# A recurrent block behind a cross-attention layer: another loop order, another end, and the last channel mixing on ScalarE and GpSimd

## The reference

```python
xa = ln(x, ln1);  sx = previous(xa) - xa
xxx = tanh((xa + sx * maa_x) @ maa_w1)             # the mixer
xk, xw, xv, xr, xg = xa + sx * (maa_stack + xxx @ maa_w2)
w = exp(-exp(time_decay + tanh(xw @ td_w1) @ td_w2));  r, k, v = ...
scan over t:  out = r . (u*k*v + s);  s = k*v + w*s  # 32 heads of 8
x1 = x + (group_norm(out) * silu(xg @ Wg.T)) @ Wo.T
xc = ln(x1, ln2);  sx2 = previous(xc) - xc           # the channel mixing
xk2 = xc + sx2 * ffn_maa_k;  xr2 = xc + sx2 * ffn_maa_r
return x1 + sigmoid(xr2 @ Wfr.T) * (square(relu(xk2 @ Wfk.T)) @ Wfv.T)
```

## Time and profile before

| | us |
|---|---|
| median of 3 runs (1112.25 to 1114.79) | 1112.68 |
| the profiled execution, its whole time | 1108.56 |
| its span | 1106.8 |
| busy: PE / DVE / ACT / POOL | 1051.5 / 888.8 / 768.4 / 607.8 |

### The profile page before, as it was taken

How to read it: one execution, slowest core, us unless ns; L and a number is a source line. 1 busy time by engine, 2 the same in 40 slices (tenths; PEclk the granted TensorE clock), 3 DMA queues, 4 the chain that set the end, 5 groups by cost and what they waited for, 6 DMA issues and landing times.

```text
span 1106.8 us, 34650 instructions
## 1 busy us (share of the span) xinstructions
PE 1051.5 (95%) x12992; PEld 878.5 (79%) x12992; DVE 888.8 (80%) x1532; ACT 768.4 (69%) x1910; POOL 607.8 (55%) x535
## 2 busy tenths in 40 slices
PE   5899999999999998999999999999999999887888
PEld 4888989888988987877788887777887777665677
DVE  5997777978777777128999999999999999999543
ACT  5677877777777776566666676666677667744774
POOL 4787888777887786024443454443454443453322
PEclk9999999999999999999999999999999999999999
DMA  9500000011111110012333331233331233303011
GB/s 331 177 4 2 0 0 2 4 41 41 41 41 46 38 38 12 1 38 70 72 81 86 86 73 45 59 81 85 85 78 38 57 83 86 86 25 99 21 38 57
DMA packets 39868, 65.01 MB, mean 59 GB/s; under 512 B 4384, under 2 KB 26208, under 8 KB 39392
## 3 DMA queue, kind: packets, MB, share of 16 engines
q1 hardware_dynamic: 39776, 63.75, 21.7%
HBM read 55.35 MB, written 8.39 MB: 58 GB/s over the span
## 4 chain that ended last, share of the span: by engine, by line
PE 84%; DVE 8%; issue 3%; ACT 3%; POOL 1%; DMA 0%; DVEq 0%; ACTq 0%; POOLq 0%
PE psum L1016 10%; PE psum L1005 10%; PE psum L353 10%; PE psum L1097 9%; PE psum L267 6%; PE psum L336 5%; PE psum L368 5%; PE psum L297 4%; PE psum L280 3%; PE psum L1056 3%; PE psum L1136 2%; PE psum L310 2%; PE psum L1169 2%; PE psum L1278 2%; DVE shared L1839 2%
## 5 line engine op out<-in xcount | busy, mean ns | idle before, releaser
L1839 DVE TENSOR_TENSOR_SCAN shared<-late_wT,shared 128x512 f32<-128x512 f32 x128 | 193.8, 1514 | 0.0
L232 POOL TENSOR_TENSOR shared<-shared,att_row_max 128x512 f32<-128x512 f32 x128 | 132.6, 1055 | 16.8 <-DVE att_row_max L564 16.8
L453 ACT ACTIVATE shared<-shared 128x512 f32<-128x512 f32 x128 | 80.5, 631 | 68.3 <-POOL shared L232 68.2
L353 PE MATMUL psum<-shared 128*128 128x128 f32 x1024 | 126.1, 277 | 0.1
L353 PEld LDWEIGHTS psum<-shared 128*128 128x128 f32 x1024 | 120.4, 193 | 0.5 <-ACT shared L462 0.5
L1016 PE MATMUL psum<-w,late_hT 128*128 128x256 f32 x512 | 120.0, 382 | 0.5 <-ACT late_hT L1396 0.5
L564 DVE TENSOR_REDUCE att_row_max<-shared 128x8 f32<-128x512 f32 x128 | 86.8, 680 | 40.9 <-POOL shared L225 40.9
L1005 PE MATMUL psum<-late_glnT,w 128*128 128x256 f32 x512 | 118.0, 383 | 1.1 <-ACT late_glnT L1387 1.0
L896 POOL TENSOR_TENSOR late_xm<-late_mixed,late_xa 128x512 f32<-128x512 f32 x64 | 78.1, 1229 | 72.6 <-DVE late_mixed L1805 72.6
L905 POOL TENSOR_TENSOR shared<-shared,late_rT 128x512 f32<-128x512 f32 x32 | 40.7, 1273 | 122.8 <-DVE shared L1839 122.8
L1005 PEld LDWEIGHTS psum<-late_glnT,w 128*128 128x128 f32 x512 | 94.7, 190 | 16.8 <-issue 3.2
(11 more groups left out here) (169 smaller groups left out, 2470.8 us busy)
## 6 DMA issues: line engine op xcount, KB each, us to landing
shared<-v_rows SPq DMA_DIRECT2D x64, 512.0 KB, 7.7
shared<-in_enc SPq DMA_DIRECT2D x64, 128.0 KB, 2.6
v_rows<-shared SPq DMA_DIRECT2D x64, 64.0 KB, 1.8
out<-x SPq DMA_DIRECT2D x16, 256.0 KB, 2.0
x<-in_x SPq DMA_DIRECT2D x7, 512.0 KB, 9.8
w<-in_w SPq DMA_DIRECT2D x2, 1024.0 KB, 17.2
shared<-in_cross_mask SPq DMA_DIRECT2D x1, 1024.0 KB, 12.3
shared<-in_w_qkv SPq DMA_DIRECT2D x1, 768.0 KB, 4.6
```

The source lines that it names most:

```text
L232: nc.gpsimd.tensor_tensor(zs, zs, peak.unsqueeze(2).to_broadcast([P, PAIRS, S]), ALU.subtract).then_inc(shifted, 1)
L353: last = nc.tensor.matmul(dst[:, half * P:(half + 1) * P], w[:, kb, c0 + half * P:c0 + (half + 1) * P], src[:, u % 2, kb, 0:P], start=(kb ...
L453: nc.scalar.activation(probs[:, u % 2, half * 4:(half + 1) * 4, :].rearrange("p r k -> p (r k)"), z[:, u % 2, half, :], ACT.Exp).then_inc( ...
L1839: nc.vector.tensor_tensor_scan(states, wT[:, u, half, :, :, :].rearrange("p j b t -> p (j b t)"), states, 0.0, ALU.mult, ALU.add).then_inc ...
```

## The change

1. **Loop order** (bodies 0 to 12). TensorE does `mixer(s+1)` right behind the gate's projection and no longer behind the head sums, the bonus sums and the output projection. VectorE does `mixer_input(s+1)` ahead of the first scan. ScalarE takes the mixer's tanh ahead of setting two groups of first states.
2. **Channel mixing in bodies 13 to 15.** For runs 0 to 5 `ch_mix` on VectorE is gone. ScalarE makes the four products (`ch_scale`), GpSimd the two additions (a `ch_mix` of its own). From run 6 on VectorE does it as before.
3. **The end.** `centre(14)`, `sum_squares(14)`, `square(14)`, the moments of run 13 and `scale(14)` move from behind the bodies into body 15. Behind the bodies the recurrence's last pieces come earlier. ScalarE makes the group norm's roots for runs 14 and 15 apart, each with two table loads, and the second `NORMS` group now takes runs 10 to 13, the last one only 14 and 15.

```diff
-        NORMS = ((0, (RUNS - 6) * CH), ((RUNS - 6) * CH, (RUNS - 3) * CH), ((RUNS - 3) * CH, RUNS * CH))
+        NORMS = ((0, (RUNS - 6) * CH), ((RUNS - 6) * CH, (RUNS - 2) * CH), ((RUNS - 2) * CH, RUNS * CH))
...
+                ch_mix(early_run(s, 0), 0)
...
+            if n == 4 and early(s):
+                ch_mix(early_run(s, 1), 1)
...
-        if there(s - 1) and not s_is(s, RUNS - 1):
-            scale(s - 1)
...
+        if there(s - 1):
+            scale(s - 1)
...
+    def ch_mix(r, u):
+        pool.wait_ge(ch_scaled, r + 1)
+        for dst in (ch_xk, ch_xr):
+            xs = dst[:, u, :, :].rearrange("p h (b t) -> p (h b) t", t=S)
+            last = nc.gpsimd.tensor_tensor(xs, xs, ch_xc[:, u, :, :, 1:S + 1].rearrange("p h b t -> p (h b) t"),
+                                           ALU.add)
+        last.then_inc(ch_mixed_ready, 1)
+
...
     ch_add(EARLY - 1, 1)
+    scale(RUNS - 1)
...
-    scale(RUNS - 2)
-    scale(RUNS - 1)
     ch_add(EARLY, 0)
...
     ch_add(EARLY + 1, 1)
-    ch_shift(EARLY + 4, 0)
-    ch_add(EARLY + 2, 0)
-    channel(EARLY + 3, 1)
-    channel_runs(pool, channel)
+    channel_runs(pool, channel, EARLY + 2)
...
+        if mixing and not early(s):
+            mixer(s + 1)
...
-        if mixing:
+        if mixing and early(s):
             mixer(s + 1)
...
-    ch_keys(EARLY, 0)
...
+    ch_keys(EARLY, 0)
+    transpose_on(RUNS - 2)
+    transpose_o(RUNS - 1)
...
-    transpose_o(RUNS - 1)
+    project_out(RUNS - 2)
...
-    ch_transpose(EARLY + 3, 1)
-    ch_keys(EARLY + 2, 0)
-    transpose_on(RUNS - 2)
-    ch_values(EARLY + 1, 1)
-    ch_receptances(EARLY + 2, 0)
-    project_out(RUNS - 2)
-    ch_transpose(EARLY + 4, 0)
-    ch_keys(EARLY + 3, 1)
...
-    ch_values(EARLY + 2, 0)
-    ch_receptances(EARLY + 3, 1)
+    channel(EARLY + 1, 1)
...
-    channel(EARLY + 3, 1)
-    channel_runs(pe, channel)
+    channel_runs(pe, channel, EARLY + 2)
...
+    def ch_scale(r, u):
+        act.wait_ge(ch_sx_ready, r + 1)
+        if r == 0:
+            act.wait_ge(down_ready, RUNS)
+        if later(r - 1):
+            act.wait_ge(ch_key_ready, r - 1)
+            act.wait_ge(ch_recept_ready, r - 1)
+        for half in range(HALVES):
+            for dst, name in ((ch_xk, "ffn_maa_k"), (ch_xr, "ffn_maa_r")):
+                last = nc.scalar.activation(dst[:, u, half, :].rearrange("p (b t) -> p b t", t=S),
+                                            ch_sx[:, u, half, :, :], ACT.Copy, scale=col(core, name, half))
+        last.then_inc(ch_scaled, 1)
+
...
-        if there(s - 1) and there(s):
+        if early(s):
             set_states(s, 2)
             set_states(s, 3)
+        if early(s):
+            ch_scale(early_run(s, 0), 0)
...
             mixer(s + 1)
+        if there(s - 1) and there(s) and not early(s):
+            set_states(s, 2)
+            set_states(s, 3)
...
+            ch_scale(early_run(s, 1), 1)
             ch_tanh(early_run(s, 0), 0)
-        if there(s - 2) and not s_is(s, RUNS - 1):
+        if there(s - 2):
             out_means(s - 2)
-        if there(s - 1) and not s_is(s, RUNS - 1):
+        if there(s - 1):
             square(s - 1)
...
-    square(RUNS - 2)
+    nc.scalar.preload_act_table_set("natural_log_exp_and_others")
+    invert_heads(RUNS - 2)
+    ch_invert(1)
+    nc.scalar.preload_act_table_set("gelu_apprx_tanh_and_others")
...
+    copy_on(RUNS - 2)
...
+    square(RUNS - 1)
+    nc.scalar.preload_act_table_set("natural_log_exp_and_others")
+    invert_heads(RUNS - 1)
+    nc.scalar.preload_act_table_set("gelu_apprx_tanh_and_others")
...
-    ch_square(EARLY + 1, 1)
-    make_stats(RUNS - 3)
-    square(RUNS - 1)
-    nc.scalar.preload_act_table_set("natural_log_exp_and_others")
-    invert_heads(RUNS - 2)
-    invert_heads(RUNS - 1)
-    ch_invert(1)
-    nc.scalar.preload_act_table_set("gelu_apprx_tanh_and_others")
-    ch_tanh(EARLY + 1, 1)
+    ch_nonlinear(EARLY + 1, 1)
+    copy_on(RUNS - 1)
...
-    copy_on(RUNS - 2)
+    make_stats(RUNS - 2)
...
-    ch_copy_in(EARLY + 4, 0)
-    ch_normalise(EARLY + 5, 1)
-    ch_square(EARLY + 3, 1)
-    copy_on(RUNS - 1)
-    ch_tanh(EARLY + 3, 1)
-    make_stats(RUNS - 2)
+    channel(EARLY + 2, 0)
+    make_stats(RUNS - 1)
...
-    ch_copy_in(EARLY + 6, 0)
-    make_stats(RUNS - 1)
...
-    ch_normalise(EARLY + 7, 1)
-    ch_nonlinear(EARLY + 5, 1)
-    channel_runs(act, channel, EARLY + 5)
+    channel_runs(act, channel, EARLY + 4)
...
+                if n == 0 and there(s + 1) and not early(s):
+                    mixer_input(s + 1)
                 scan(s, u, n)
...
-                if there(s + 1):
+                if there(s + 1) and (early(s) or not there(s)):
                     mixer_input(s + 1)
...
-                    ch_mix(early_run(s, 0), 0)
...
-                if there(s - 1) and not s_is(s, RUNS - 1):
+                if there(s - 1):
...
-                if early(s):
-                    ch_mix(early_run(s, 1), 1)
...
-                if there(s - 1) and not s_is(s, RUNS - 1):
+                if there(s - 1):
...
-    centre(RUNS - 2, 0)
...
-    sum_squares(RUNS - 2)
...
+    apply_gate(RUNS - 2, 0)
+    sum_squares(RUNS - 1)
+    ch_shifts(1)
+    add_residual(RUNS - 2)
...
-    sum_squares(RUNS - 1)
...
-    ch_shifts(1)
-    apply_gate(RUNS - 2, 0)
...
+    apply_gate(RUNS - 1, 1)
...
-    add_residual(RUNS - 2)
+    add_residual(RUNS - 1)
...
-    apply_gate(RUNS - 1, 1)
-    ch_finish(EARLY + 2, 0)
-    add_residual(RUNS - 1)
-    ch_mix(EARLY + 5, 1)
-    ch_finish(EARLY + 3, 1)
+    channel(EARLY + 3, 1)
+    channel(EARLY + 4, 0)
...
-    ch_mix(EARLY + 6, 0)
```

More of the change, by code:

```diff
@@ L787, in late_phase @@
                     "value_ready rv_ready out_ready stored out_sum_ready out_mean_ready stats_ready norm_logged norm_rstd "
-                    "norm_ready").split()
+                    "norm_ready scaled").split()
         (ch_xn_ready, ch_xnT_ready, ch_xc_ready, ch_sx_ready, ch_mixed_ready, ch_key_ready, ch_relu_ready, ch_kk_ready,
          ch_recept_ready, ch_rr_ready, ch_value_ready, ch_rv_ready, ch_out_ready, stored, out_sum_ready, out_mean_ready,
-         stats_ready, norm_logged, norm_rstd, norm_ready) = semaphores(nc, ctx, *(f"ch_{n}" for n in ch_names))
+         stats_ready, norm_logged, norm_rstd, norm_ready, ch_scaled) = semaphores(nc, ctx, *(f"ch_{n}" for n in ch_names))
         v_loaded = semaphores(nc, ctx, *(f"late_v_part{q}_loaded" for q in range(SUMS)))
-        NORMS = ((0, (RUNS - 6) * CH), ((RUNS - 6) * CH, (RUNS - 3) * CH), ((RUNS - 3) * CH, RUNS * CH))
+        NORMS = ((0, (RUNS - 6) * CH), ((RUNS - 6) * CH, (RUNS - 2) * CH), ((RUNS - 2) * CH, RUNS * CH))
         att = attention(core, ctx)
@@ L824, in early_run, with channel_runs @@
             return CH * (s - (RUNS - 3)) + i
-        def channel_runs(eng, body, start=EARLY + 4):
+        def channel_runs(eng, body, start):
             for s in range(start, RUNS):
```

## The result

| | median us | range, runs | profiled execution | its span |
|---|---|---|---|---|
| before | 1112.59 | 1112.25 to 1114.79, 4 | 1108.56 | 1106.8 |
| after | 1105.97 | 1105.26 to 1106.77, 4 | 1106.15 | 1104.4 |

The ratio is 0.9939, 95% interval 0.9922 to 0.9957: 6.6 us less. The forecast was 1106.2. The number is right, the sum behind it is not: a gain of 4.2 us that it put at nothing and 4.5 us that it counted and that did not come (parts 3, 4 and 6) cancel. That they cancel is luck.

The account below looks back on a forecast made before the run. TensorE was taken to bound the loop bodies, VectorE close behind, with TensorE gaps from body 13 on. Terms -0.6 - 0.3 - 1.5 - 2.8 - 2.2 + 0.9 = -6.5 us gave 1102.1 profiled, 1106.2 median; range 1101 to 1113.

Parts of the forecast that it names:

- Part 3: Body 15: mixing of run 4 ready earlier, values of run 5 come earlier despite added centring and squares; -1.5 us.
- Part 4: Behind the bodies, up to run 15's output projection: TensorE idle 3.3 us, then no wait, 31.5 for 34.3; -2.8 us.
- part 6: TensorE's clock behind the new 3.3 us wait may be halved: 0 to 1.7 us lost, +0.9 taken.
- part 1: Loop order, bodies 0 to 12: TensorE has no gap, so an earlier mixer cannot shorten a body; 0.
- Part 2: Channel mixing off VectorE in bodies 13 and 14: VectorE then waits for the values, so only -0.6 and -0.3 us.
- Part 5: The last stretch: run 13's normalisation wait goes, new waits of 0.7 and 1.3 us come; net -2.2 us.
- rival B: Relief eaten: GpSimd's additions hold body 15's scans, the end waits as before; about -1.4 us, 1111.3; chance 0.22.
- rival C: Slower by the loop: the later first scan makes VectorE the bound in 13 bodies; 1119.2 us; chance 0.10.
- rival A: Relief arrives in full in bodies 13 to 15, as VectorE's busy share suggests; 1098.3 us; chance 0.12.

Follow-up runs that it names:

- run 13: Not a follow-up: one of the kernel's own numbered channel runs; the change moves its moments into body 15.
- run 14: Not a follow-up: one of the kernel's own numbered channel runs; in after TensorE waits 3.58 us ahead of its output projection.
- run 15: Not a follow-up: one of the kernel's own numbered channel runs; it is centred on VectorE behind the bodies.
- sums_apart: The changed kernel with the bonus product moved between the mixer and the head sums on TensorE in bodies 0 to 12; 1109.66 us, ratio 0.9968 to before.
- run 7: Not a follow-up: one of the kernel's own numbered channel runs; VectorE does its channel mixing behind the bodies, 2.66 us in after.
- mix_back: The changed kernel with the channel mixing of runs 0 to 5 back on VectorE as one operation; 1106.38 us, ratio 0.9938 to before.
- gate_first: The changed kernel with VectorE centring run 15 and gating run 14 ahead of mixing run 7, behind the bodies; 1099.98 us, ratio 0.9876 to before.
- old_end: The changed kernel with the end and normalisation groups as before, loop order and channel mixing new; 1106.85 us, ratio 0.9954 to before.

## Why the prediction was right in number and wrong in its parts

The step that failed is part 1: it put the loop order at 0, and it is worth 4.15 us. What the prediction argued for, parts 2 to 6, gave 1.8 us in the traces (0.84 + 0.92) and 3.4 in the medians (sums_apart, which has all of it without the loop's gain). Both lie in the range of rival B (0.5 to 4), and B's sign came too: from body 13 on, values(5) are 0.84 us earlier, less than 1. So beside the loop B described the outcome better than the forecast.

Each part against the traces from body 0 on:

| part | predicted | in the traces |
|---|---|---|
| 1 loop order | 0 | -4.15 |
| 2 mixing, bodies 13 and 14 | -0.9 | -0.75 |
| 3 body 15 | -1.5 | -0.1 |
| 4 behind the bodies, with 6 the clock | -2.8 + 0.9 | +1.2 |
| 5 the last part | -2.2 | -2.1 |
| sum | -6.5 | -5.9 |

**Part 1 failed** in its first sentence: "TensorE has no gap there, so an earlier mixer cannot shorten a body." It took a product's length for fixed. It depends on its neighbours: 1.82 us or 1.72 for the same eight products, and 32-column products overlap. The trace of before held the hint: start to start, this projection takes 1.82 us and the equal one two groups ahead (L1097 at 826.63) 1.73; I compared only busy time. The question asked instead, what VectorE loses by the later scan, was answered rightly: the loop stayed TensorE's, and rival C did not come. The Trainium skill has the rule that I left out, "TensorE: Matmul & The Clock Gate", section "Part 3: Packing small matmuls — row/col tiling": products on different 32-wide tiles of the array run at once. The interleaved rows of this case agree (0.13 us a body). That a neighbour of other width can also cost 0.10 us stands on the runs here alone.

**Part 2 was right.** VectorE waits for the values (2.73 and 2.74 us in bodies 13 and 14), and keys of run 1 come 0.40 us earlier than the loop's gain explains, 0.35 more in body 14. VectorE's busy share was no measure: rival A did not come. ScalarE's four products took 1.71 us, 1.7 was taken.

**Part 3 was mis-sized.** Keys of run 4 come 0.7 us earlier from the start of the body, and the head sums give it back: the additions stand ahead of the reads in GpSimd's queue. I counted what additions do to scans, not that they hold the reads. And beside scans the reads were longer, which I had not counted either. It is rival B's result in this one place, by the queue and by the meetings together.

**Part 4 came out 3.1 us worse, with part 6.** Values(5) to the output projection of run 14 took 11.5 us for 10.7 predicted, mostly the mixing of run 7, which took 2.66 us beside GpSimd's addition and not 1.7. The wait was 3.58 for 3.3. The table loads took 1.28 us each, and the next instruction starts 1.29 to 1.30 us behind the load's start, with no drain between, as the sum had it (the earlier trace rows shows the load alone; in before's trace the next instruction starts at 1045.24). But part 6 gave the clock 0.9 us and 1.7 at worst, and it cost 2.9: TensorE works at half its clock for six microseconds here, for three in the earlier trace rows. In mix_back it cost 1.5, within part 6's bounds. So the set of products took 35.5 us for 34.3 before. In the new order this set ends with the receptances that end at 1062.9 and not, as part 4 says, with `project_out(15)`, which starts at 1055.42; the 20.8 us are those of the whole set. gate_first shows the price of wait and clock together: 5.9 us in that stretch. Without them the new end is worth 6.8 us (65.15 against old_end's 71.95), more than parts 4 and 5 gave it together.

**Part 5 was right**, though its waits were 0.74 and 1.01 for 0.7 and 1.3.

The sum's 1102.1 for the profiled execution was missed by 4.1 us: it took 1106.15, 0.2 above the median. Before's profiled execution was the odd one. Adding the 4.1 us back for the median, the last step of the sum, was right for the comparison of medians.

## What to carry to other kernels

An engine that is busy for the whole of a loop can still be sped up by order: compare the same product start to start beside different neighbours, and put products that write only 32 columns side by side. When work leaves a full engine, look who waits next: here the receiver's queue and the values' chain took back most of it. After a wait of TensorE price the slow clock behind it too, and first look whether the awaited step merely stands behind others in its queue; one exchange there was worth nearly as much as the whole change (6.0 and 6.6 us).
